# Two stacked transformer layers on one core: x loaded first, the slot norm moved to a later step, the second layer's first weights loaded during the first layer

## What is computed

```python
# layer 0, both on xn = layernorm(x)
x = x + attention0(xn) + soft_moe(xn)
#   attention0: 16 heads of 8, a shared rotary part of 32, causal softmax over 512 tokens
#   soft_moe:   xn and 512 slot embeddings are RMS-normed; logits = xn @ sn.T;
#               dispatch = softmax over tokens, combine = softmax over slots;
#               8 experts (128 -> 512 -> 128, gelu) on 64 slots each
# layer 1, both on xn = layernorm(x)
x = x + attention1(xn) + moe(xn)
#   attention1: 16 heads of 64, keys and values from a rank-128 latent, causal softmax
#   moe:        16 experts, the best 8 of each token weighted, and one shared expert
```

## Time and profile before

| | |
|---|---|
| three timed runs | 3251.52, 3255.03, 3257.3 us; median 3255.03 |
| profiled execution | 3248.36 us, its span 3246.6 us |
| mean granted TensorE clock | 0.990 |
| busy share of the span | PE 96%, DVE 62%, ACT 50%, POOL 39% |
| DMA | 259.86 MB in all |
| layer 0 / layer 1 | the boundary is at 1246.24 us |

### The profile page before, as it was taken

How to read it: one execution, slowest core, us unless ns; L and a number is a source line. 1 busy time by engine, 2 the same in 40 slices (tenths; PEclk the granted TensorE clock), 3 DMA queues, 4 the chain that set the end, 5 groups by cost and what they waited for, 6 DMA issues and landing times.

```text
span 3246.6 us, 62545 instructions
## 1 busy us (share of the span) xinstructions
PE 3103.6 (96%) x23476; PEld 1674.8 (52%) x23476; DVE 2005.2 (62%) x3829; ACT 1632.8 (50%) x3433; POOL 1279.7 (39%) x1223
## 2 busy tenths in 40 slices
PE   4999999999999994999999999999999999999999
PEld 2565555655555652445555554554554554554554
DVE  5666666656666653666666666666666666666664
ACT  2666656556666663444444444444444444444443
POOL 1333333323333321444444444444444444444444
PEclk9999999999999996999999999999999999999999
DMA  4211122221222113332432432432432442432431
GB/s 116 53 50 50 50 59 63 62 50 50 62 50 52 50 47 107 105 96 76 108 103 71 108 104 71 108 105 70 108 103 72 108 107 68 108 107 68 108 105 43
DMA packets 239643, 259.86 MB, mean 80 GB/s; under 512 B 27248, under 2 KB 228080, under 8 KB 230640
## 3 DMA queue, kind: packets, MB, share of 16 engines
q1 hardware_dynamic: 217680, 239.12, 28.1%
q10 hardware_dynamic: 21664, 16.73, 1.7%
HBM read 107.91 MB, written 21.50 MB: 40 GB/s over the span
## 4 chain that ended last, share of the span: by engine, by line
PE 56%; DVE 2%; DMA 1%; SPq 1%; ACT 1%; POOL 0%; issue 0%; DVEq 0%; POOLq 0%; ACTq 0%
PE l_ps_out L1548 9%; PE l_ps_any L1585 7%; PE l_ps_any L1448 6%; PE l_ps_any L1450 6%; PE l_ps_any L1449 6%; PE l_ps_exp L1531 4%; PE l_ps_exp L1533 4%; PE l_ps_any L1591 3%; PE l_ps_any L1506 3%; PE l_ps_sum L1559 2%; PE l_ps_any L1571 2%; PE l_ps_exp L1535 2%; DMA l_spread<-route_scratch 1%; SPq L1089 1%; PE l_ps_any L1511 1%; PE l_ps_any L1442 1%
## 5 line engine op out<-in xcount | busy, mean ns | idle before, releaser
L1161 POOL TENSOR_TENSOR l_hw<-l_hidden,l_spread 128x512 f32<-128x512 f32 x256 | 325.5, 1277 | 761.5 <-DMA l_spread<-route_scratch 200.2
L614 DVE TENSOR_REDUCE neg_max<-ps_any 128x1 f32<-128x384 f32 (+3 forms) x704 | 417.4, 634 | 269.1 <-PE ps_any L728 264.6
L1249 ACT ACTIVATE l_probs<-l_ps_exp 128x512 f32<-128x512 f32 x640 | 376.9, 596 | 377.4 <-PE l_ps_exp L1535 288.0
L501 ACT ACTIVATE probs<-ps_exp 128x512 f32<-128x512 f32 x640 | 349.3, 602 | 155.2 <-PE ps_exp L743 154.5
L442 POOL TENSOR_SCALAR_AFFINE_SELECT probs<-probs 128x512 f32<-128x512 f32 x256 | 159.4, 634 | 597.4 <-ACT probs L501 597.4
L1370 DVE TENSOR_REDUCE l_neg_max<-l_ps_any 128x2 f32<-128x768 f32 (+2 forms) x384 | 316.4, 863 | 86.4 <-PE l_ps_any L1511 86.0
L1531 PE MATMUL l_ps_exp<-l_q_a,l_k_a 128*128 128x512 f16 (+3 forms) x1024 | 306.4, 300 | 0.3 <-ACT l_probs L1249 0.2
L1548 PE MATMUL l_ps_out<-l_probs,l_v 128*64 128x512 f32 (+3 forms) x2048 | 303.1, 438 | 0.0
L1533 PE MATMUL l_ps_exp<-l_q_b,l_k_b 65*128 65x512 f16 (+3 forms) x1024 | 295.4, 300 | 0.0
L726 PE MATMUL ps_any<-k_st,q_st 120*128 120x128 f16 (+3 forms) x1024 | 252.8, 304 | 36.2 <-DMA k_st<-stack_scratch 35.2
L1256 ACT ACTIVATE l_tanh<-l_ps_any 128x512 f32<-128x512 f32 x272 | 162.4, 597 | 208.2 <-PE l_ps_any L1450 113.7
(11 more groups left out here) (234 smaller groups left out, 6276.1 us busy)
## 6 DMA issues: line engine op xcount, KB each, us to landing
l_spread<-route_scratch SPq DMA_DIRECT2D x64, 1024.0 KB, 5.5
l_q_a<-l_q_hi SPq DMA_DIRECT2D x256, 128.0 KB, 2.4
l_q_b<-l_q_lo SPq DMA_DIRECT2D x128, 128.0 KB, 2.4
l_k_a<-l_k_hi SPq DMA_DIRECT2D x128, 128.0 KB, 2.4
l_k_a<-l_k_lo SPq DMA_DIRECT2D x128, 128.0 KB, 2.4
l_k_b<-l_k_hi SPq DMA_DIRECT2D x128, 128.0 KB, 2.4
q_st<-rot_hi SPq DMA_DIRECT2D x64, 128.0 KB
k_st<-rot_hi SPq DMA_DIRECT2D x64, 128.0 KB
```

Of the source, the lines that this page charges most:

```text
L501: nc.scalar.activation(probs[:, n % 2, u], ps_exp[:, (10 * g + u) % 3], ACT.Exp, scale=float(HD0 + DR) ** -0.5).then_inc(exp_done.sem, 1)
L614: nc.vector.tensor_reduce(neg_max[:, n % 2, heads[0]:heads[0] + k, t], src, AX.X, ALU.max, negate=True).then_inc(drained["dve"], 1)
L1161: nc.gpsimd.tensor_tensor(dst, hidden[:, k % 2], spread[:, c % 2, n % CHUNK], ALU.mult).then_inc(hw_ok.sem, 1)
L1249: nc.scalar.activation(probs[:, n % 2, u], ps_exp[:, (5 * p + u) % ST_BANKS], ACT.Exp, scale=float(HD1) ** -0.5).then_inc(exp_done.sem, 1)
```

## The change

Layer 0: x of the first batch is SP's first load; eight of the small loads stay on SP, ten go to ACT's queue, ahead of w1 and w2. PE waits for both lists. The slot norm becomes a step `snT` on DVE, POOL, PE and ACT, eight steps ahead of the first logits; DVE's ident and mask follow the first `scale`. v_aug is cleared by POOL.

Layer 1: an `Early` buffer in SBUF holds the raw masks, w_kvd, gate_w, w_q, w_kvu and w_g, and w_out; SP loads them in layer 0, at the load of batch 8. probs, x_res and weight of layer 1 now lie in that buffer. x is SP's first load; w_g is split with the first ones (`split_in`), w_u alone is late. k_b is cleared by POOL.

```diff
@@ layer0_program
-    return [x for x in steps if 0 <= x[1] < batches]
+    steps = [x for x in steps if 0 <= x[1] < batches]
+    first = min(steps.index(x) for x in (("logits_s", 0, 0), ("logits_c", 0, 0)))
+    return steps[:first - 8] + [("snT", 0, 0)] + steps[first - 8:]
@@ layer0
+        loads = [(ident[:], a["ident"]), (w_kvd[:], a["L0_attn_W_kv_down"]), (w_q[:], a["L0_attn_W_q"]),
+                 (w_k[:], a["L0_attn_W_k_up"]), (cos[:], a["cos"]), (sin[:], a["sin"]), (w_v[:], a["L0_attn_W_v_up"]),
+                 (mask[:], a["mask"])]
+        act_loads = rope + [
+            (gamma[:], a["L0_ffn_norm_gamma"].partition_broadcast(P)),
+            (slot_nat[:], a["L0_ffn_slot_embeds"].rearrange("e s d -> (e s) d").rearrange("(m p) d -> p m d", p=P)),
+            (slot_gamma[:], a["L0_ffn_slot_norm_gamma"].partition_broadcast(P)), (w_o[:], a["L0_attn_W_o"])]
@@ sync
+            sp.dma_start(x_in[:], a["L0_attn_x"][0].rearrange("(t p) d -> p t d", p=P)).then_inc(x_loaded.sem, 16)
             for dst, src in loads:
                 sp.dma_start(dst, src).then_inc(loaded, 16)
...
+                if name == "load" and b == batches // 2:
+                    for dst, src in early.loads:
+                        sp.dma_start(dst, src).then_inc(early.loaded, 16)
+                if name == "load" and b:
@@ scalar
+            for dst, src in act_loads:
+                act.dma_start(dst, src).then_inc(act_loaded, 16)
             for dst, src in late_loads:
                 act.dma_start(dst, src).then_inc(late_loaded, 16)
-            act.wait_ge(prep_pe, 1)
-            nc.scalar.activation(snT[:], ps_any[:, 0], ACT.Copy).then_inc(prep_act, 1)
-            act.wait_ge(prep, 13)
-            act.wait_ge(loaded, all_loaded)
@@ vector
-            nc.vector.memset(v_aug[:], 0.0).then_inc(prep, 1)
             nc.vector.memset(k_st[K_ROPE:P], SHIFT).then_inc(prep, 1)
-            dve.wait_ge(loaded, all_loaded)
...
+                if at == after_scale:
+                    dve.wait_ge(loaded, all_loaded)
+                    dve.wait_ge(act_loaded, all_act)
+                    nc.vector.tensor_copy(ident_h[:], ident[:]).then_inc(prep, 1)
+                    nc.vector.tensor_copy(mask_h[:], mask[:]).then_inc(prep, 1)
+                if name == "snT":
+                    slots_normed()
@@ tensor
             pe.wait_ge(loaded, all_loaded)
+            pe.wait_ge(act_loaded, all_act)
...
+                if name == "snT":
+                    pe.wait_ge(slots_ok, 9)
+                    turned("snT0", [slot_n[:, c] for c in range(4)])
@@ layer1
+        loads = [(ident[:], a["ident"]), (bias[:], a["L1_ffn_expert_bias"].partition_broadcast(P))]
...
+        for w, name in ((w_u_in, "up"), (w_d, "down")):
             late_loads += [(w[:, 0:E1], a[f"L1_ffn_w_{name}"]), (w[:, E1], a[f"L1_ffn_shared_{name}_w"])]
...
-                    (w_kvu[:].rearrange("p c s n -> p c (s n)"), w_kvu_in)]
-        split_late = [(w_g, w_g_in), (w_u, w_u_in)]
+                    (w_kvu[:].rearrange("p c s n -> p c (s n)"), w_kvu_in), (w_g, w_g_in)]
+        split_late = [(w_u, w_u_in)]
@@ layer1, scalar
-            act.wait_ge(loaded, all_loaded)
+            act.wait_ge(early.loaded, early.all)
@@ layer1, vector
-            nc.vector.memset(k_b[HD1:P], SHIFT).then_inc(prep, 1)
...
+            dve.wait_ge(early.loaded, early.all)
             dve.wait_ge(loaded, all_loaded)
@@ class Early
+        self.loads = [(masks[HD1 * r:HD1 * r + HD1, half], a["maskT"][HD1 * half:HD1 * half + HD1])
+                      for r in range(2) for half in range(2)]
+        self.loads += [(masks[:, 2], a["maskT"]), (w_kvd, a["L1_attn_w_kv_down"]), (gate, a["L1_ffn_gate_w"]),
+                       (w_q, a["L1_attn_w_q"]), (w_kvu, a["L1_attn_w_kv_up"]), (w_g[:, 0:E1], a["L1_ffn_w_gate"]),
+                       (w_g[:, E1], a["L1_ffn_shared_gate_w"]),
+                       (self.w_out[:], a["L1_attn_w_out"].rearrange("(k p) d -> p k d", p=P))]
```

More of the change, by code:

```diff
@@ L196, in by_act0, with layer0 @@
     name, _, n = step[:3]
[L197 removed]
+    return name in ("snT", "xnT", "xfT", "ckv", "v", "slots", "attnT", "out", "soft_s", "soft_c", "hidden", "turn_max") or (
         name in ("dispatch", "combine") and n % 2 == 0)
[L201 removed]
+def layer0(nc, a, x1_dram, batches, early):
     with ExitStack() as ctx:
@@ L1119, in _ @@
             pool.wait_ge(prep_pool, 1)
-            pool.wait_ge(loaded, all_loaded)
+            nc.gpsimd.memset(k_b[HD1:P], SHIFT).then_inc(prep_pool, 1)
+            pool.wait_ge(prep_pool, 2)
             for step in program:
@@ L1429, in _ @@
             pe.wait_ge(loaded, all_loaded)
-            pe.wait_ge(prep, 13)
+            pe.wait_ge(prep, 12)
+            pe.wait_ge(prep_pool, 2)
+            pe.wait_ge(early.loaded, early.all)
             pe.wait_ge(weights_lo, len(split_in))
@@ L1595, in _, with __init__ @@
                     turned(f"outT{b}", [acc[:, b % 2, t * P:t * P + P] for t in range(TB)])
+class Early:
+    def __init__(self, ctx, nc, a):
+        self.stage = ctx.enter_context(nc.sbuf_tensor("stage", [P, STAGE], F32))
+        self.w_out = ctx.enter_context(nc.sbuf_tensor("l1_w_out", [P, PAIRS, D], F32))
+        self.loaded = ctx.enter_context(nc.semaphore("early_loaded"))
+        sizes = [H * HD1, 2 * H * HD1, 3 * P, P, E1, EXPERTS * D]
+        starts = [sum(sizes[:k]) for k in range(len(sizes))]
+        self.raw = [self.stage[:, x:x + n] for x, n in zip(starts, sizes)]
+        w_q, w_kvu, masks, w_kvd, gate, w_g = self.raw
+        masks = masks.rearrange("p (s k) -> p s k", s=3)
+        w_g = w_g.rearrange("p (e d) -> p e d", d=D)
+        self.loads = [(masks[HD1 * r:HD1 * r + HD1, half], a["maskT"][HD1 * half:HD1 * half + HD1])
[4 more added lines that the diff above has]
+                       (self.w_out[:], a["L1_attn_w_out"].rearrange("(k p) d -> p k d", p=P))]
+        self.all = 16 * len(self.loads)
 def build(nc, a, out, batches):
     x1_dram = nc.dram_tensor("x1_scratch", [batches, T, D], F32, kind="Internal").ap()
-    layer0(nc, a, x1_dram, batches)
-    layer1(nc, a, x1_dram, out, batches)
+    with ExitStack() as ctx:
+        early = Early(ctx, nc, a)
+        layer0(nc, a, x1_dram, batches, early)
+        layer1(nc, a, x1_dram, out, batches, early)
 def constants():
```

109 lines of the change are left out of this document (53 added, 56 removed).

## The result

The changed kernel took 3265.47 us (median of 20 runs, 3256.61 to 3269.94), the kernel before 3252.49 beside it: ratio 1.0035, interval 1.0027 to 1.0042. It is **slower by 0.35%**. I had forecast no change (3250.1, range 3240 to 3259), with 0.06 on slower. The profiled execution took 3260.71 us, span 3259.0, against a span of 3246.6 before: +12.4.

A forecast was written before the change was run, and what follows sets the result against it. PE was taken to bound the kernel, with gains only where it stands still: the start and the layer boundary. Terms -6.2 + 2.7 + 6.1 - 8.0 - 1.2 + 1.7 = -4.9 gave 3250.1 us, range 3240 to 3259.

The forecast's parts named there:

- The start: Start of layer 0: x first and slot norm moved, xnT copied at 25.5 once ACT's hold ends; -6.2 us, range 2.7 to 7.5.
- 3.48 MB at the rate of w1 alone: Start of layer 0: the w1 and w2 data to pass before ACT's hold ends take 10.3 us, ending at 19.7.
- The rival that ACT isn't held: Start of layer 0: b2 issues don't wait, xnT copied at about 11.5; -18 in place of -6.2, 3238 us, chance 0.08.
- The slot norm: Batch 0, behind max(0,1,0): PE waits for slot_n until 61.9 and adds four transposes; +2.7 us, bounds 1.5 and 3.5.
- The early loads: Batch 7: x_in behind twelve issues lands 7.4 us late, delaying PE's first hidden product; +6.1 us, from 0 to 9.
- the twelve issues cost about 0.55 each: SP's queue in batch 7: early loads at about 0.55 us per issue put x_in's issue at 598.
- The clock: Behind PE's stop in batch 7: 3.4 us at the 1.2 GHz level, half of it lost; +1.7 us.
- the stop of 6.1 us in batch 7 should do the same: Batch 7: PE's stop draws 3.4 us of low clock, like the 1.99 us stop at 964.90; +1.7 us.
- the argument that PE is packed here: After the stops in batches 0 and 7 PE is packed, but at 1290 to 1300 was busy 5.40 of 10 us.
- The boundary and the first experts: Start of layer 1: stats 8.0 us earlier, -8.0; w_g's split gone from PE's wait before the experts, -1.2.
- the small loads would land by +3: Layer boundary: small loads pass the large ones, 5.8 us more gained; sum -10.7, 3244 us, chance 0.07 as a rival.
- The rival for slower: Batches 0 and 7: each new PE stop draws 10 us of low clock; sum +3.4, 3258.5 us, chance 0.12.

The follow-up runs named there:

- the run with nine loads: Against the change: nine of the twelve early loads ahead of x_in of batch 8, three behind x_in of batches 9 to 11; 3254.21 us, ratio 1.0008 to before.

## Why the prediction was wrong

- **The start, -6.2 forecast, -3.4 measured.** The mechanism was right: ACT held by its b2 issues to the end. The size failed in the step "3.48 MB at the rate of w1 alone". The data of w1 did start at 9.5. But the hold ended only when 0.65 MB of the queue were still to come, where the prediction took the 0.97 of the earlier trace rows, so 0.32 MB more had to pass; and they passed slower than w1 alone, with SP's and ACT's small loads landing until 12.8. The hold ended at 21.8, not 19.7. The table load is at 26.34 and not "near 24". The rival that ACT isn't held is out. Some of the shortfall is scatter: in the eight other kernels with this start the first max stood at 43.3 to 45.4, here at 46.08. And the term took the hold as given; the run with b2 behind the copy of k shows that 16.6 us more lay there.
- **The slot norm, +2.7 forecast, +5.7 measured.** The stop was sized well (2.1 against 1.87). The missing part is the clock: 6.8 us at the lower level, of which 0.9 in the stop, so 3.0 lost. I had given this stop a clock cost only in the rival.
- **The early loads, +6.1 forecast, a stop of 7.5.** Mis-sized by 1.4: "the twelve issues cost about 0.55 each", but the five of the masks took 0.88 each, 1.6 us more in all.
- **The clock, +1.7 forecast, 8.6 measured in batch 7, and 3.0 in batch 0.** This is the step that failed: "the stop of 6.1 us in batch 7 should do the same", taken from the earlier trace rows, a stop of 1.99 us with 3.4 us behind it. A stop of 1.99 was no measure for one of 6.1. The runs show in its place 20.5 us at the lower level behind the 7.5 us, and over all executions 13 us behind a stop of 3.1 and 21 behind one of 7.5. The earlier trace rows had a stop of 7.39 us with 10 behind it, the nearer row in size; I set it aside by the argument that PE is packed here, which the run with nine loads refutes. Its own price, 10 us, would have been too low as well.
- **The boundary and the first experts, -9.2 forecast, -7.2 measured.** The boundary came as forecast: DVE at +9.5 against +8.8, PE's transposes 7.6 us earlier against 8.0. The experts' wait fell by 2.34 us (the prediction had 2.42, less half for the clock). By the first product of the experts the gain was 11.7 us, at +36.6 against +48.4, more than the 9.2 forecast. But 4.5 us of it were lost again by the end of layer 1, and no row shows where. It is no chance of one execution of the change: in all ten kernels with this boundary layer 1 took 1991.9 to 1997.4 us, on average 6.5 less than the 2000.4 before, of which there is one execution only. The prediction also read from a rule of the Trainium skill (DMA: Bandwidth & Descriptors, section on queues, rings and completion order: an engine drains a packet of typically 9 to 17 descriptors from one queue before it goes to the next) that the small loads would land by +3. Bias landed at +9.5, as one packet for one of the earlier trace rows gives. This doesn't refute the rule, from which the +3 did not follow: turns of equal length on both queues pass as many of one as of the other too.
- **The rival for slower** named the right mechanism and place, priced the stretch at 10 us (measured 20.5 and 6.8), and said it passes 0.2% "only with stretches of some 13 us". By its own rule that was met. Its chance of 0.12 was too small, and the 0.06 on slower with it.

Put together: -3.4 + 5.7 - 0.9 + 15.9 + 2.3 - 7.2 = +12.4, the difference of the spans. The 2.3 between batch 9 and the boundary was not tested by itself. That the sum closes says nothing of the terms, since the pieces are cut from the same two spans.

## What to carry to other kernels

When a load is put ahead of one that somebody needs soon, the cost is the stop it makes **plus** what the clock takes behind it. Here turning the order round, or spreading the loads one behind each urgent one, made the same loads free. When an engine both issues DMAs and computes, read how long its last issues take: a hold that was hidden becomes the path as soon as the wait beside it is removed. Price a stop of PE from a row of the same length in the same sort of work, and where there is none, keep the whole span between the nearest rows in the range.

## What was not expected of the hardware

- In one execution, after a stop of 3.1 us, PE ran for 20.5 us at 1.2 GHz although the trace shows it busy for 20.00 of 20.00 us in that stretch (some 13 us on average over all executions of that kernel); after 5.5 us it was 27.3, after 7.5 us 20.5 to 23.9 (the change and three kernels with the same stop in batch 7), after 8.8 us 30.7. A stop of 1.99 us at 964.9 had 3.4 us behind it, and two in batch 0, of 1.61 and 1.87 us with 0.60 us of work between them, 6.8 us. The work behind these long stretches is always the same, first the 128x64 hidden products and then the rest of the batch; whether other work would have ended them sooner was not tried.
- A DMA load of 0.72 of 16 engines, 225 GB/s, left PE's clock at 1.00.
- A DMA issue can hold its engine for long. The first b2 issue, behind the 4.19 MB of w1 and w2 on its own queue, took 12.4 us on ACT, and 13.8 on SP once the loads were moved there. On ACT it was let go when 0.65 MB of that queue were still to come (0.97 before).
